# Softmax reciprocals of an attention layer taken for two query tiles at a time

## The reference, cut to what matters

```python
# layer 0, x is (8, 512, 32, 32): n = 1024 tokens, 8 heads of 64 channels
hn  = group_norm(x, gn1_scale, gn1_bias)
qkv = einsum('bchw,oc->bohw', hn, w_qkv) + b_qkv
wgt = softmax(einsum('bct,bcs->bts', q * scale, k * scale), axis=-1)
a   = einsum('bts,bcs->bct', wgt, v)
x   = x + group_norm(einsum('bchw,oc->bohw', a, w_proj) + b_proj, gn2_scale, gn2_bias)
# layer 1: one-head attention over 512 channels on the same x, RMS-normalised q, k, v,
# output projection, (x + h) / sqrt(2)
```

## Time and profile before

| | |
|---|---|
| time, median of 3 runs | 3530.38 us (3525.94 to 3533.14) |
| the profiled execution | 3528.0 us, span 3526.2 us |
| TensorE busy | 3462.6 us, 98% of the span |
| VectorE, ScalarE, GpSimd busy | 59%, 52%, 31% |
| granted TensorE clock, mean | 0.998 |
| share of TensorE in the chain that ended last | 87% |

### The profile page before, as it was taken

One profiled execution on the slowest core, in us unless ns is written; L12 is line 12 of the kernel. 1 busy time (PEld: TensorE's weight loads), 2 busy tenths in 40 slices (PEclk: granted clock), 3 DMA queues, 4 the chain that ended last, 5 costly groups with the idle time before them and its releaser, 6 DMA issues.

```text
span 3526.2 us, 52658 instructions
## 1 busy us (share of the span) xinstructions
PE 3462.6 (98%) x17360; PEld 2835.9 (80%) x17360; DVE 2077.1 (59%) x3388; ACT 1825.4 (52%) x3074; POOL 1083.3 (31%) x947
## 2 busy tenths in 40 slices
PE   7999999999999999999999999999999999999999
PEld 3888788887888788887878878788787887888878
DVE  4677446773377734786347854478444884457742
ACT  3577126762278522784237832378323882247822
POOL 0245213442034410354104531145211452114521
PEclk9999999999999999999999999999999999999999
DMA  8512215312244113341033311342203422142210
GB/s 310 157 39 58 108 43 138 74 48 84 66 115 96 41 69 97 85 96 72 36 121 81 76 72 43 114 96 61 84 37 109 96 61 84 43 133 65 60 48 24
DMA packets 63520, 294.41 MB, mean 83 GB/s; under 512 B 9201, under 2 KB 9457, under 8 KB 52465
## 3 DMA queue, kind: packets, MB, share of 16 engines
q1 hardware_dynamic: 63216, 290.65, 28.1%
HBM read 158.49 MB, written 31.46 MB: 54 GB/s over the span
## 4 chain that ended last, share of the span: by engine, by line
PE 87%; issue 6%; DVE 3%; ACT 2%; POOL 2%; DMA 0%; SPq 0%; ACTq 0%; DVEq 0%; POOLq 0%
PE big L430 29%; PE tps L529 14%; PE big L556 12%; PE ops L542 12%; PE ops L702 10%; PE big L626 6%; PE big L473 1%; PE ops L430 1%; ACT PB L827 1%; PE big L594 1%; DVE XA L1247 1%; POOL XA L967 1%; DVE HL L1252 0%; DVE small L1175 0%; PE big L465 0%
## 5 line engine op out<-in xcount | busy, mean ns | idle before, releaser
L957 POOL TENSOR_SCALAR PB<-PB,small 128x1024 f32<-128x1024 f32 x576 | 648.1, 1126 | 1304.3 <-DVE small L1181 1293.4
L833 ACT ACTIVATE PT<-tps 128x512 fp32r<-128x512 f32 x1088 | 601.2, 597 | 251.7 <-PE tps L529 248.5
L1186 DVE TENSOR_TENSOR PT<-tps,PT 128x512 fp32r<-128x512 f32 x1088 | 693.1, 678 | 39.0 <-ACT PT L833 38.6
L1175 DVE TENSOR_REDUCE small<-big 128x1 f32<-128x1024 f32 x512 | 624.8, 1220 | 63.2 <-PE big L556 59.9
L529 PEld LDWEIGHTS tps<-ident,PB 128*128 128x128 f32 x4608 | 527.1, 140 | 125.0 <-DVE PT L1186 56.0
L529 PE MATMUL tps<-ident,PB 128*128 128x128 f32 x4608 | 618.0, 275 | 8.9 <-DVE PT L1186 6.1
L827 ACT ACTIVATE PB<-big,small 128x1024 f32<-128x1024 f32 x512 | 572.2, 1118 | 73.1 <-DVE small L1175 70.2
L542 PE MATMUL ops<-PT,VT 128*128 128x512 f32 x2048 | 599.3, 415 | 0.0
L556 PE MATMUL big<-ST 128*128 128x512 f32 x2048 | 555.4, 393 | 10.9 <-ACT PB L827 10.9
L556 PEld LDWEIGHTS big<-ST 128*128 128x128 f32 x2048 | 382.1, 188 | 101.8 <-ACT PB L827 19.9
L542 PEld LDWEIGHTS ops<-PT,VT 128*128 128x128 f32 x2048 | 346.2, 189 | 47.0 <-DVE PT L1186 5.0
(11 more groups left out here) (157 smaller groups left out, 4659.2 us busy)
## 6 DMA issues: line engine op xcount, KB each, us to landing
ST<-ST SPq DMA_DIRECT2D x384, 256.0 KB, 4.9
W<-d_qk SPq DMA_DIRECT2D x32, 1024.0 KB, 5.2
XA<-in_x SPq DMA_DIRECT2D x8, 2048.0 KB, 7.7
X<-in_x SPq DMA_DIRECT2D x8, 2048.0 KB, 10.6
W<-d_wp SPq DMA_DIRECT2D x8, 2048.0 KB, 12.2
W<-d_g SPq DMA_DIRECT2D x8, 2048.0 KB, 12.2
W<-d_m SPq DMA_DIRECT2D x8, 2048.0 KB, 7.7
W<-d_u SPq DMA_DIRECT2D x8, 2048.0 KB, 10.3
```

The costliest lines, as they stand in the source:

```text
L833: act_fn(pt_slot(u, s)[:, 0, :], tps[n % 2][:], ACT.Copy).then_inc(s_pt_hi, 1)
L957: nc.gpsimd.tensor_scalar(PB[:, i, :], PB[:, i, :], rinv[:, i:i + 1], 1.0, ALU.mult, ALU.mult)\
L1175: V.tensor_reduce(negmax[:, i:i + 1], tile(("s", 4 * u + tb))[:], axis=AX.X, op=ALU.max, negate=True).then_inc(s_row_max, 1)
L1186: V.tensor_tensor(pt_slot(u, s)[:, 1, :], tps[n % 2][:], pt_slot(u, s)[:, 0, :].bitcast(f32), ALU.subtract).then_inc(s_pt_ready, 1)
```

## The change

The reciprocal of an even tile is no longer taken by itself. That of an odd tile becomes one instruction over two columns, its own and the one before it, and it raises the semaphore by two.

```diff
                 def recip(u, tb):
                     i = 4 * (u % 2) + tb
-                    dve.wait_ge(s_exp_done, b * 72 + 4 * u + tb + 1)
-                    V.reciprocal(rinv[:, i:i + 1], rowsum[:, i:i + 1]).then_inc(s_recip_done, 1)
+                    if tb % 2:
+                        dve.wait_ge(s_exp_done, b * 72 + 4 * u + tb + 1)
+                        V.reciprocal(rinv[:, i - 1:i + 1], rowsum[:, i - 1:i + 1]).then_inc(s_recip_done, 2)
```

## The result

The changed kernel takes 3576.06 us (3573.23 to 3576.78, 4 runs) against 3528.16 us (3525.43 to 3533.14, 4 runs) for the kernel before: a ratio of 1.0132, 95% interval 1.012 to 1.0144. It is slower by 42 to 51 us. The profiled execution took 3573.2 us with a span of 3571.4, which is 45.2 more than before; 38.6 had been worked out, 3568 forecast.

The account below looks back on a forecast made before the run. TensorE was taken to bound the kernel. Border waits of 5.29 us per image plus 0.07 for the pair less 0.54 from VectorE made 4.82, times eight 38.6 us; 3568 us was forecast, range 3551 to 3579.

Parts of the forecast that it names:

- TensorE bounds: TensorE, busy 98% of the span with 87% of the chain, pays in full for whatever makes it wait.
- the unit's border: Where a unit's transposes await GpSimd's last multiplication: the unit is complete 1.12 us later, 5.29 us per image in all.
- Two multiplications in one piece, handover of 0.13: GpSimd's two multiplications after the pair take 2.24 us without a gap; TensorE's transposes start 0.13 us after they end.
- The borders one by one: Ten units lose 0.31 to 0.41, unit 6 1.37, unit 15 1.12 us; units 0, 1, 4, 5, 8, 9 nothing.
- slack of 0.87 us: At unit 11's border, the time the multiplication's end may move later before TensorE's transposes wait for it.
- VectorE's gift: One reciprocal less before the subtractions shortens TensorE's wait by 0.06 us in steps 6, 8, 10: 0.54 per image.
- Catching up: Rival: other engines catch up after TensorE's wait, so only units 6 and 15 lose; 15.6 us, 3546; chance 0.09.
- The sign that I had named for being wrong: At the border, the fourth tile's exponential coming earlier after TensorE's wait than it does now.
- The slack can't be used: Rival: something unseen needs the present distance, so every one of the ten borders loses 1.12, unit 6 1.37; 3618; chance 0.05.
- Not slower: Rival: GpSimd's second multiplication at the border is hidden and VectorE's relief counts, at most 4.3 us; 3526; chance 0.04.
- the mechanism's own 3560 to 3576: Bounds in us for the border mechanism alone, from the multiplications' gap, VectorE's saving and the late start's cost.
- a gap of 0.09 between the two multiplications: GpSimd's two multiplications at the border might lie 0.09 us apart instead of 0, adding 6.5 us.

Follow-up runs that it names:

- high_pair: Against the kernel before, only tiles 2 and 3 of a unit share a reciprocal, tiles 0 and 1 have one each; ratio 1.0124.
- low_pair: Against the kernel before, only tiles 0 and 1 of a unit share a reciprocal, tiles 2 and 3 have one each; ratio 0.9999.
- pair_half: The changed kernel, with the multiplication of a unit's fourth tile covering only the first 512 of 1024 columns; ratio to the kernel before 1.0033.
- all_four: Against the changed kernel, one reciprocal over four columns per unit, at the fourth tile's place; ratio to the kernel before 1.1071.
- pair_scale25: The changed kernel with x's third scaling after tile 25 in place of tile 26; ratio to the kernel before 1.0081.
- pair_one: The changed kernel, but a pair's reciprocal raises the semaphore by one and GpSimd counts pairs; ratio to the kernel before 1.0099.
- late_signal: The kernel before with all 64 one-column reciprocals, but only the odd tile's raises the semaphore, by two; ratio 1.0139.

## Why the prediction was right, point by point

- **TensorE bounds, and the place is the unit's border.** Right: high_pair has the loss, low_pair has none. The third tile's multiplication is what became late.
- **Two multiplications in one piece, handover of 0.13.** Right, 2.23 and 0.13. They lie closer than I took: the second starts 1.10 us behind the first.
- **The borders one by one.** From scores to scores, units 3, 7, 11 and 12 grew by 0.37 to 0.40 us (0.31 worked out), 13 and 14 by 0.37 to 0.39 (0.37), units 2 and 10 by 0.53 less the 0.06 that step 12 gained, 0.47 (0.41), unit 6 by 1.48 (1.37), unit 15 by 1.19 (1.12); units 0, 1, 4, 5, 8 and 9 don't wait. pair_half, all_four and pair_scale25 move these borders as a slack of 0.87 us says.
- **What was missing.** Eight of the ten terms are 0.06 to 0.11 too small, mostly for one reason: an increment of two makes the wait an instruction of its own, 0.07 us. I had priced the pair by its columns (it takes 160 ns where I took 163) and not its signal. pair_one gives it back, at units 13 and 14 too.
- **VectorE's gift.** Steps 6, 8 and 10 are 0.05 to 0.07 shorter, as worked out, and late_signal takes it away again. The Trainium skill (VectorE: DVE Perf Modes, the TRN2 errata) had 0.06 by its table and 0.16 by its measurement for one instruction: the runs agree with the table's number as the distance from one instruction to the next.
- **The rivals.** Catching up fell, but not quite: in units 13 and 14 the fourth exponential had ended 0.07 later in relation to the scores than in units 11 and 12, and most of that is gone behind the new waits, which is why these two terms needed no correction. The sign that I had named for being wrong, a fourth exponential that comes earlier after TensorE's wait, thus did show there, by some 0.06. My reading against this rival was loose as well: ScalarE's 0.53 us of waiting stand ahead of the third tile's exponential, not of the fourth's. In all_four nothing is caught up. "The slack can't be used" is refuted by pair_half. "Not slower" would have needed the pair to end within 0.87 us; in unit 11 it ends 1.2 later.
- **The size.** 5.34 per image against 4.82; the 0.07 at ten borders less the two that caught up is 0.56, and covers the difference of 0.52. So two errors of opposite sign partly cancelled, which is luck: with an increment of one (pair_one) the growth is 4.55, 0.27 under my sum, half of it in units 13 and 14, which then take 0.29 to 0.31 in place of 0.37. Outside the attention stage the changed kernel lost 2.8 us that I had not considered. The median of 3576.06 lies at the upper end of the mechanism's own 3560 to 3576, and what I had set that end by, a gap of 0.09 between the two multiplications, is not there; the cost of the signal and the clock took its room.

## What to carry to other kernels

When two small instructions are merged, price the consumer first: ask when the first result was used, and what the queue of the engine that uses it holds from then to the next point where somebody waits. An instruction saved on an engine that isn't waited for is worth the start-to-start distance that it frees there (here 0.06 us of 0.156), and only in steps where somebody waits for that engine. Count a merged signal so that the increment stays one.

## What the runs showed of the hardware that I had not expected

**A semaphore increment of two costs an instruction.** The 0.07 us above. The Trainium skill (Trainium Kernel Development and Optimization, Key Constraints) says that compute semaphores are raised by 1. Here they can be raised by two, at that price.

**TensorE's clock falls for a moment after a wait, in some images and not in others.** Each image has one wait of 1.8 us in the output stages. TensorE's timeline there, in the third image of the kernel after, where the clock fell:

```profile
1240.37 0.65 PE L626 MATMUL big<-HH,W 128*128 128x512 f32 x1 [1.83 <-DVE HL L1253]
1240.82 0.63 PE L626 MATMUL big<-HL,W 128*128 128x512 f32 x1
```

and the same place of the kernel before, where it didn't:

```profile
1226.81 0.50 PE L626 MATMUL big<-HH,W 128*128 128x512 f32 x1 [1.82 <-DVE HL L1252]
1227.14 0.40 PE L626 MATMUL big<-HL,W 128*128 128x512 f32 x1
```

The matmuls follow each other at 0.43 us instead of 0.23. The stretch in the kernel after (columns as above):

```profile
1240.60:1243.90 3.30, 3.30 (x9) 2.52 (x9) 2.49 (x2) 0.00 (x0) 3.30 (x2) 0.50 0.05 9
```

The wait is the same; the granted clock was 0.50 for some eight matmuls, 1.6 us lost. That happened in three of eight images in the kernel before and in five after, 3.3 us more, and with 0.5 less elsewhere it is the 2.8 us outside the attention stage. It doesn't follow the length of the attention stage: low_pair, where that is shorter, has a span 3.5 us over before. Nor does it look like chance from execution to execution alone: the mean granted clock was 0.995 to 0.997 in the four of the kernel after and 0.998 to 0.999 in the five of pair_scale25, whose profile has two such falls. The number seems to go with the kernel's timing, so a few us of the differences in time above are of this kind and not of the attention stage. What decides whether the clock falls was not tried.
